# Two 8-wide attention layers: scores that follow the maxima after 13 half steps instead of 16, copies of the maxima on two queues, and a bias that leaves the matrix engine

## The reference, cut to what matters

```python
q = (xn @ Wq.T + bq) * scale                  # 256 queries, 16 heads of 8
s = q_h @ k_h.T                               # 256 x 512 for each head
s = s + slopes_h * key_position  (layer 2)    # and a mask: layer 2's own per item,
                                              # layer 3's a triangle times a padding
p = exp(s - max(s)) ; o = (p @ v_h) / (sum(p) + sink)
x = x + tanh(gate) * (o @ Wo.T + bias)        # bias in layer 3 only
```

## Time and profile before

| what | us |
|---|---|
| median of 3 runs (lowest, highest) | 1580.84 (1578.31, 1586.22) |
| the profiled execution | 1591.15 |
| its span, first to last instruction | 1589.4 |
| PE busy | 1389.2 (87%) |
| DVE busy | 1062.8 (67%) |
| ACT busy | 782.4 (49%) |
| POOL busy | 652.1 (41%) |
| layer 2's attention in the trace | about 815 to 1108 |
| layer 3's attention in the trace | about 1260 to 1565 |

### The profile page before, as it was taken

How to read it: one execution, slowest core, us unless ns; L and a number is a source line. 1 busy time by engine, 2 the same in 40 slices (tenths; PEclk the granted TensorE clock), 3 DMA queues, 4 the chain that set the end, 5 groups by cost and what they waited for, 6 DMA issues and landing times. The chain is left out here.

```text
span 1589.4 us, 30026 instructions
## 1 busy us (share of the span) xinstructions
PE 1389.2 (87%) x10374; PEld 748.5 (47%) x10382; DVE 1062.8 (67%) x3273; ACT 782.4 (49%) x1112; POOL 652.1 (41%) x504
## 2 busy tenths in 40 slices
PE   6999878559999999999339999998999579999994
PEld 4444365525666666666222333333677423333332
DVE  4988753266676666764688777773566787777755
ACT  3777632336565565654113555555433115555552
POOL 4767523315676666768631311210510342233001
PEclk8999988858999999999666999999999859999996
DMA  4555644435342343400043433500300024221201
GB/s 143 206 213 215 242 155 141 133 119 213 146 154 80 111 149 146 153 8 1 17 110 80 87 69 86 104 17 2 94 1 1 13 44 73 39 39 39 38 2 30
DMA packets 88041, 147.60 MB, mean 93 GB/s; under 512 B 15924, under 2 KB 61135, under 8 KB 84310
## 3 DMA queue, kind: packets, MB, share of 16 engines
q1 hardware_dynamic: 84558, 116.94, 25.8%
q10 hardware_dynamic: 1824, 25.17, 4.1%
q0 software_dynamic: 1520, 3.68, 0.9%
HBM read 93.66 MB, written 45.11 MB: 87 GB/s over the span
## 5 line engine op out<-in xcount | busy, mean ns | idle before, releaser
L1883 DVE CUSTOM_DVE_ANT_0 a_junk<-a_psM,a_madd 128x512 bf16<-128x512 f32 x512 | 332.0, 683 | 90.6 <-issue 87.7
L1828 ACT ACTIVATE a_probs<-a_psE 128x1024 f32<-128x1024 f32 x256 | 262.3, 1024 | 215.2 <-PE a_psE L1717 214.3
L2290 DVE TENSOR_REDUCE a_mx<-a_psM 128x1 f32<-128x512 f32 x236 | 148.2, 669 | 124.8 <-PE a_psM L2114 124.8
L1717 PE MATMUL a_psE<-a_maddT,res_identb 64*128 64x512 bf16 x1024 | 222.0, 387 | 2.1
L1694 PE MATMUL a_psM<-narrow_k_op,narrow_q_op 57*128 57x512 bf16 (+1 forms) x512 | 153.6, 415 | 44.4 <-DVE a_mx L1883 21.5
L2251 ACT ACTIVATE a_probs<-a_psE 128x1024 f32<-128x1024 f32 x128 | 130.9, 1025 | 86.2 <-PE a_psE L2136 82.9
L1728 PE MATMUL a_psO<-a_probs,narrow_values 128*32 128x256 f32 x2048 | 163.2, 392 | 2.6 <-ACT a_probs L1828 1.1
L2084 POOL TENSOR_TENSOR a_half_sum<-a_probs 128x1024 f32<-128x1024 f32 x64 | 150.9, 2358 | 33.7 <-ACT a_probs L2251 33.4
L2132 PE MATMUL a_psE<-a_qT,a_kT 64*128 64x256 f32 x1024 | 134.2, 382 | 0.0
L204 POOL TENSOR_SCALAR res_xn<-res_X,res_mv,n_rstd 128x128 f32<-128x128 f32 x28 | 24.1, 869 | 251.1 <-DVE n_rstd L190 251.1
L2148 PE MATMUL a_psO<-a_probs,a_values 128*64 128x256 f32 x1024 | 124.6, 385 | 0.8 <-ACT a_o_raw L2235 0.8
(11 more groups left out here) (361 smaller groups left out, 2514.3 us busy)
## 6 DMA issues: line engine op xcount, KB each, us to landing
wide_k<-a_k_stage SPq DMA_DIRECT2D x32, 512.0 KB, 3.1
a_k_part<-wide_k SPq DMA_DIRECT2D x64, 256.0 KB, 3.2
wide_v<-a_v_stage SPq DMA_DIRECT2D x24, 512.0 KB, 3.8
a_kT<-wide_k ACTq DMA_DIRECT2D x6, 2048.0 KB, 8.2
a_values<-wide_v ACTq DMA_DIRECT2D x6, 2048.0 KB, 8.9
keys<-a_parts SPq DMA_DIRECT2D x96, 64.0 KB
narrow_q_op<-a_y_parts SPq DMA_DIRECT2D x192, 32.0 KB
narrow_k_op<-keys SPq DMA_DIRECT2D x30, 192.0 KB
```

The lines of the kernel that those rows point to most:

```text
L1717: return pe.matmul(psE[s % 2][:, j, :, :], res.identb[group, :], maddT[r][group, s % 2 * 2:s % 2 * 2 + 2, :], start=False, stop=last, skip ...
L1828: act.activation(probs[:, head:head + 2, k:k + 2, :], psE[s % 2][:], ACT.Exp).then_inc(exped, 1)
L1883: dve.tensor_tensor_reduce(junk[j][:], psM[j][:], madd[r][:, t, :], 1.0, -3.0e38, ALU.add, ALU.max, mx[r][:, max_place(h, t):max_place(h, ...
L2290: dve.tensor_reduce(mx[r][:, at:at + 1], max_bank(2 * p + t, j, first), AX.X, ALU.max).then_inc(max_read, 1)
```

## The change

It does five things in `narrow_attention`.

1. **The scores run 13 half steps behind the maxima** (`LAG = 13`) instead of 16. Half step s of step v now scores head pair s + 3 of item v - 1 for s below 13, and head pair s - 13 of item v from there on. Step 0 has scores in its last three half steps, and step 8 has only 13 half steps. All slots move with it.
2. **The copies of the maxima** are issued half by SP (row group 0) and half by POOL (row group 1), three DMAs each, with semaphores of their own. POOL's program is now, for each item: three copies, three copies, the masks of item v + 2; before, it held masks alone.
3. **The first item's queries** are issued half by SP and half by ACT, and `y` has four buffers, so that ACT no longer waits for DVE.
4. **The bias of layer 3** is spread over 128 rows by one product, scaled by ACT into `bias_tile`, and added to `res.X` by POOL in 16 additions; the products of one row in `project` go.
5. PE waits for the masks at an item's first score, and at the start of layer 3 for `row_done`, which DVE sets.

```diff
-        y = [ph.sb(f"y{i}", [P, CHUNK]) for i in range(2)]
+        y = [ph.sb(f"y{i}", [P, CHUNK]) for i in range(NCHUNK)]
...
-        MAX_SLOTS, READ_SLOT, OUT_SLOT, BACK_SLOT, PROJECT_SLOT, V_SLOT = (10, 1), 3, 5, 7, 9, 12
-        STATS_SLOT = PROJECT_SLOT - 1
+        LAG = 13
+        MAX_SLOTS, READ_SLOT, OUT_SLOT, BACK_SLOT, PROJECT_SLOT, V_SLOT = (8, 0), 1, 3, 5, 7, 11
+
+        def scored_now(v, r, s):
+
+            return (v - 1, (r - 1) % RING, s + HEADS - LAG) if s < LAG else (v, r, s - LAG)
+        STATS_SLOT = LAG - B + 1
...
+        def maxima_rows(eng, r, half, j, landed):
+            n = HALF // 2
+            for c in range(3):
+                at = j * GROUP_ROWS + rows + c
+                eng.dma_start(q_op[r][at:at + 1, half * n:(half + 1) * n, :].rearrange("o h (t q) -> o (h t) q", q=P),
+                              max_parts[half][j * n * QT:(j + 1) * n * QT, c, :]).then_inc(landed[half], 16)
...
                 def maxima(v, r, half):
                     sp.wait_ge(max_split, (2 * v + half + 1) * n_split)
+                    maxima_rows(sp, r, half, 0, max_in)
...
-                load_queries(0, 0)
+                sp.wait_ge(split, 4)
+                query_rows(sp, 0, 0, 0)
...
+                for u in range(2):
                     masks(u, u, 0, True)
+                if cfg.q_bias:
+                    pool.wait_ge(bias_tiled, 1)
+                    for t in range(NTILE):
+                        pool.tensor_tensor(res.X[:, t, :], res.X[:, t, :], bias_tile[:], ALU.add).then_inc(bias_added, 1)
+                for v in range(B):
+                    pool.wait_ge(max_split, (2 * v + 1) * n_split)
+                    maxima_rows(pool, v % RING, 0, 1, max_in_other)
+                    pool.wait_ge(max_split, (2 * v + 2) * n_split)
+                    maxima_rows(pool, v % RING, 1, 1, max_in_other)
+                    if v + 2 < B:
+                        masks(v + 2, (v + 2) % RING, (v + 2) // RING, v + 2 < RING)
...
                 pe.wait_ge(biased, NCHUNK)
+                if cfg.q_bias:
+                    pe.wait_ge(row_done, 1)
+                    pe.matmul(psX[:, 0:D], res.ones[0:1, :], bias_row[:], start=True, stop=True).then_inc(bias_spread, 1)
...
-                        if cfg.q_bias:
-                            if t == 0:
-                                pe.wait_ge(row_done, 1)
-                            pe.matmul(y, res.ones[0:1, :], bias_row[:], start=True, stop=False)
-                        last = pe.matmul(y, AT[:, t * P:(t + 1) * P], wo[:], start=not cfg.q_bias, stop=True)
+                        last = pe.matmul(y, AT[:, t * P:(t + 1) * P], wo[:], start=True, stop=True)
...
+                    for s in range(HEADS if take_max else LAG):
+                        w, at, es = scored_now(v, r, s)
+                        take_exp = after_first or s >= LAG
...
+                        quad, t = es // QUAD - 1, es % QUAD
                         if quad >= 0 and take_exp:
+                            weigh(w, at, quad, t, first)
+                        if quad < 0 and (inner or w >= 1):
+                            weigh(w - 1, (at - 1) % RING, QUADS - 1, t, False)
...
+                act.wait_ge(split, 4)
+                query_rows(act, 0, 0, 1)
+                if cfg.q_bias:
+                    act.wait_ge(bias_spread, 1)
+                    act.activation(bias_tile[:], psX[:, 0:D], ACT.Copy, scale=res.gates[:, cfg.gate:cfg.gate + 1]).then_inc(bias_tiled, 1)
```

More of the change, by code:

```diff
@@ L1547, in narrow_attention, with query_rows @@
         pad_taken, pad_mixed = ph.sem("pad_taken"), ph.sem("pad_mixed")
-        MAX_SLOTS, READ_SLOT, OUT_SLOT, BACK_SLOT, PROJECT_SLOT, V_SLOT = (10, 1), 3, 5, 7, 9, 12
-        STATS_SLOT = PROJECT_SLOT - 1
-        n_split = 4
+        LAG = 13
[3 more added lines that the diff above has]
+        STATS_SLOT = LAG - B + 1
+        n_split = 4
+        def query_rows(eng, u, r, j):
+            n, b = u // 2, u % 2
+            for part, (first, end) in enumerate(RUNS):
+                for c in range(first, end):
+                    at = j * GROUP_ROWS + c * HEAD_E
+                    eng.dma_start(q_op[r][at:at + HEAD_E], y_parts[n][j * GROUP_ROWS:(j + 1) * GROUP_ROWS, part, b * S:(b + 1) * S]).then_inc(loaded[r], 16)
         def steps(eng, step):
@@ L1585, in load_queries @@
                 def load_queries(u, r):
[L1586 to L1592, removed]
+                    sp.wait_ge(split, 4 * (u // 2) + 4)
+                    for j in range(2):
+                        query_rows(sp, u, r, j)
                 def maxima(v, r, half):
                     sp.wait_ge(max_split, (2 * v + half + 1) * n_split)
[L1597 to L1602, removed]
+                    maxima_rows(sp, r, half, 0, max_in)
                 load_masks(0, 0)
                 load_keys(0, 0)
-                load_queries(0, 0)
+                sp.wait_ge(split, 4)
+                query_rows(sp, 0, 0, 0)
                 load_masks(1, 1)
@@ L1697, in turn_maxima @@
                 def turn_maxima(v, r, half):
+                    if cfg.q_bias and r == 0 and half == 0:
+                        pe.wait_ge(bias_tiled, 1)
                     pe.wait_ge(max_read, (v * HEADS + (half + 1) * HALF) * QT)
@@ L1734, in step @@
                 def step(v, r, turn, inner=False):
[L1735 to L1736 removed]
+                    take_max, after_first, finish = inner or v < B, inner or v >= 1, inner or v >= 2
                     if take_max:
[L1738 removed]
+                        if not inner and v == 0:
                             pe.wait_ge(nb.first_keys, 16 * n_keys)
@@ L1740, in step @@
                         pe.wait_ge(loaded[r], 16 * (n_loads * (turn + 1) - (n_keys if r == 0 else 0)))
-                    if take_exp:
-                        pe.wait_ge(masked, v * 2)
+                    if after_first:
                         pe.wait_ge(v_out, 2 * v)
-                    for s in range(HEADS):
+                    for s in range(HEADS if take_max else LAG):
+                        w, at, es = scored_now(v, r, s)
+                        take_exp = after_first or s >= LAG
+                        first = not inner and v == (0 if s >= LAG else 1)
@@ L1749, in step @@
                         if take_max:
                             for j in range(2):
-                                maximum(v, r, s, j, first and v == 0)
+                                maximum(v, r, s, j, not inner and v == 0)
                         if take_exp:
[L1753 to L1757, removed]
+                            pe.wait_ge(half_masked, w * HEADS + es + 1)
@@ L1758, in step @@
+                            mask(at, es, 1, 0, True)
+                            mask(at, es, 0, 1, True).then_inc(scored, 1)
+                        quad, t = es // QUAD - 1, es % QUAD
                         if quad >= 0 and take_exp:
[L1759 to L1765, removed]
+                            weigh(w, at, quad, t, first)
```

60 lines of the change are left out of this document (31 added, 29 removed).

## The result

The changed kernel takes 1589.58 us, the median of 20 runs (1584.67 to 1594.35). The kernel before, run on the same chip, takes 1583.72 (20 runs, 1578.31 to 1589.57). The ratio is 1.0035, with a 95% interval of 1.0024 to 1.0047: slower, by 5.5 us. The forecast was 1599, 18 us or 1.2% slower than 1580.84. The sign was right, the size some three times too large.

The account below looks back on a forecast made before the run. PE was taken to set the pace, DVE in step 0. Terms without the clock summed to -1.1 us; the clock's +19.6 made +18.5, giving 1599 us against the median of 1580.84, range 1577 to 1620.

Parts of the forecast that it names:

- The clock: +19.6: PE's clock falls to 1.2 GHz behind seven of 14 new waits, 2.8 us each: +19.6 us; chance 0.50.
- the signs that the prediction named: ACT's late `OT` copy, 3.2 to 3.4 us between exponentials, PE idle 1.6 to 1.7 us, low clock in single windows, among others.
- three to eleven: Failure test: the prediction fails if the clock falls in fewer than three or more than eleven of the new waits.
- Read-out: +14.5: Steps 2 to 8, both layers: PE idles 1.67 us for ACT's copy out of `psO`, partly given back; 7.25 us per layer.
- DVE's 0.74: Given back in six of seven waits per layer, as DVE catches up while PE idles: -0.74 us each.
- Bias: -8.2: Half step behind `project`, layer 3: one-row products go, 1.03 us x 8 items; POOL's 16 additions hidden.
- PE's wait for the row: +1.1: Start of layer 3: PE waits for the bias row and multiplies it before the first maxima; +1.1 us (0 to 1.5).
- Start of layer 2: -1.4: Queries come sooner, but DVE's first maximum still follows its last cut, so only 1.40 us can go.
- Three half steps: -7.1: Each layer's front loses three half steps of maxima alone, 4.15 us; 0.6 comes back at the end; net -3.55 per layer.
- Copies on two queues: 0: Maxima copies on SP and POOL land before PE needs them, hidden: 0 us.
- The fifth rival: POOL's copies come late, 1.4 us for each of 16 first halves, 22 us more: 1602 or 1621; chance 0.08.
- The fourth rival: PE's new wait for the read-out is not there, gets in ahead or is hidden: 1565, faster by 1.0%; chance 0.10.

Follow-up runs that it names:

- Experiment 3: Changed kernel with 14 needless products on PE ahead of its wait for the copy out of psO; 1581.69 us, ratio 0.9983 to the kernel before.
- experiment 1: Changed kernel with ACT's copy out of psO one half step sooner, behind the exponential of half step 0; 1569.55 us, ratio 0.9907 to the kernel before.
- experiment 2: Kernel before with only ACT's copy out of psO moved later, behind the exponential of half step 4 instead of 3; 1606.65 us, ratio 1.0147.
- experiment 5: Kernel before with only the bias of layer 3 moved as in the change; 1576.86 us, ratio 0.9959.
- experiment 6: Changed kernel with psO copied out behind half step 0's exponential, and second queue, first-query and bias edits undone; 1607.2 us, ratio 1.0121 to the kernel before.
- experiment 7: Changed kernel with psO copied out behind half step 0's exponential and all maxima copies on SP's queue; 1598.93 us, ratio 1.0046 to the kernel before.
- experiment 8: Kernel before, lag still 16 half steps, with only the maxima copies split over SP's and POOL's queues; 1583.22 us, ratio 1.0001.
- experiment 4: Changed kernel with 7 needless products on PE ahead of its wait for the copy out of psO; 1582.51 us, ratio 0.9997 to the kernel before.
- the early copy: Changed kernel with psO copied out behind half step 0's exponential; with DVE's steps 2 to 7 also written out, 1569.71 us, ratio 0.9880 to the kernel before.

## Why the prediction was wrong in size

The failed step is **"The clock: +19.6"**, the last term of the sum, and in it "seven falls of 14: 7 x 2.8". The mechanism was right: the signs that the prediction named came, and the falls were five, inside its three to eleven.

- *Clock.* Seven falls at 2.8 us were forecast on top of the one that was there. The profile has five in all, and four of them last 3.4 us and cost 1.3 each: 4 x 1.3 + 2.8 = 8.0, or 5.2 more than before. Experiment 3, which takes the low clock behind these places away, measures 6.6, give or take 3. So the term was 13 to 14 us too large, in number and above all in price: 2.8 was read from one row, a 6.8 us fall, and taken for all. The length was also misread a little: the idle 1.61 and 1.38 us of the earlier trace rows are sums over a window, and the longest single pieces there are 1.37 and 1.15 us, both shorter than the new wait. Where the row and the page of the Trainium skill (TensorE: Matmul & The Clock Gate, Why this matters for your kernels) were weighed, neither was right: idle pieces much shorter than those that the page warns of do lose the clock, but not in half of the cases and not for 2.8 us.
- *Read-out: +14.5.* The mechanism, its place and its length were right (1.68 measured for 1.67; experiments 1 and 2 move the time by 20 and 23 us with one number). The net size is 18.1 by layer 3's items; over both layers, from first reduction to last exponential, the profile of experiment 1 is 18.8 us shorter, 1.1 of them clock, which leaves 17.7. DVE's 0.74 is indeed hidden in the wait, since the gap without it would be 2.31 and not 1.57, but the next half step then takes 1.78 instead of 1.57, 0.2 us of what was given back.
- *Bias: -8.2*, and *PE's wait for the row: +1.1.* The half step behind `project` went from 3.23 to 2.21 as forecast. The wait costs 1.65 (1.82 us from the last cut to the first reduction, 0.17 before), just over its bound. Together -6.6; experiment 5 measures -6.8, with an interval of 3 either way. POOL's additions took 6.61 us, from 1283.00 to 1289.61, ahead of its first copies at 1292.98: hidden.
- *Start of layer 2: -1.4.* Measured -1.47, from the end of the last cut (826.53) to the first reduction (826.46).
- *Three half steps: -7.1.* From first reduction to first exponential it is 26.11 us before and 21.92 after in layer 3: 4.19 less, for 4.15; in layer 2 21.48 after, 4.63 less. With what it costs later in the layer, layer 3 of experiment 6 saves 2.6 us, for 3.55: -5.3 in two layers like it. In layer 2 this was not measured alone, since there the copies come late.
- *Copies on two queues: 0.* PE waited 2.1 us in all for them in layer 2, 1.2 before, so the net is right to 1 us. The fifth rival, late copies on POOL, was priced at 22 us and did not come: POOL issues 0.53 us each beside DVE's reductions too, 0.3 us behind the cut in most items. SP was forecast 1.8 us late; it is 2.8 and 1.8 late at the first halves of items 1 and 3 and on time at the others. But the 0 hid a pair: the shorter lag makes the copies late at a price of some 20 us, low clock included, and the second queue takes this away (experiments 6, 7 and 8). The sum was right and its two halves were not seen.

With the measured sizes: -1.5 + 1.65 - 7.1 - 8.2 + 17.7 + 5.2 = +7.8, and +9.6 with -5.3 for the lag, against 5.5 by the ratio (3.8 to 7.4). Where the other 2 to 4 us are is not shown; single profiles of one kernel differ by more (that of the kernel before is 7.4 us over its median). The parts need not add either: without the read-out's wait SP starts the first half's copies late in five of seven items, with it in two. Without the clock the forecast had -1.1, and 5.5 less 5.2 to 6.6 is +0.3 to -1.1. That this agrees is in part luck, since the read-out's term was 3 us too small and 2 to 4 us of gain have no name. One more part of the miss was the starting point: the median of before over 20 runs is 1583.7, not 1580.8. That the measured 1589.6 lies inside the stated range owes something to this, and to a range as wide as 43 us.

The fourth rival, that the wait is not there, was forecast at 1565 and given 0.10. It was wrong for this kernel, but one other number in the slots takes the wait away: 1569.55.

## What to carry to other kernels

When a schedule is shifted, ask of every slot which single buffer it frees and what stands ahead of it in its engine's order. Here the lag moved by three half steps and the copy out of `psO` by two, so that it stood behind one exponential more, and this took back more than the rest had gained (experiment 1). A term of zero is worth a second look when two edits meet in it; shorten a lag only together with the queue that must keep up with it. And price a falling clock from several falls, not from one.

## What the runs showed of the hardware that I had not expected

- The low clock inside these layers comes in two lengths, 3.4 and 6.8 us, at 1.2 GHz instead of 2.4, and the short one costs 1.3 us of time, the long one 2.8. The same wait of 1.68 us lost the clock in 5 of 14 cases in one execution; in experiment 2, one of 1.69 us did in 2 of 14.
- An idle piece of 0.7 us in its place, after 0.9 us of needless products, lost it in none of 14 (experiment 4).
- The length of the idle piece alone does not decide. At DVE's branch, in the one profile of experiment 5, PE stood for 1.45 us in layer 2 and the clock stayed at 1.00, and for 1.12 us in layer 3 and it fell:

```profile
976.60 0.39 PE L1698 MATMUL a_psM<-narrow_k_op,narrow_q_op 57*128 57x512 bf16 x1 [1.45 <-DVE a_mx L1894]
...
977.00:980.00 3.00, 2.79 (x30) 1.01 (x30) 2.47 (x12) 1.31 (x2) 0.00 (x0) 1.00 0.03 8
980.00:983.00 3.00, 2.77 (x34) 0.89 (x26) 2.56 (x13) 1.72 (x3) 0.00 (x0) 1.00 0.01 2
...
1421.89 0.39 PE L1698 MATMUL a_psM<-narrow_k_op,narrow_q_op 48*128 48x512 bf16 x1 [1.12 <-DVE a_mx L1894]
...
1424.00:1427.00 3.00, 3.00 (x22) 0.85 (x24) 2.37 (x10) 1.20 (x2) 2.76 (x4) 0.50 0.02 3
```

- With the needless products in the waits, the clock also stayed at 1.00 behind the branch in layer 3, where PE stood for 0.98 and 0.23 us; in experiment 1, with 1.19 and 0.23 us idle at that place, it fell to 0.50, and in experiment 2, with 1.21, it stayed. Why is open.
- DVE's steps written out cost 0.14 us per middle item of layer 3 with the early copy (30.92 for 30.78) and 0.01 in the kernel before. One branch cost 1.7 to 1.8 us where no low clock followed (33.63 for 31.92 in experiment 4, 35.31 for 33.55 in experiment 2).
